# Attention on one Trainium2 core: half of the second pair additions move to VectorE, and the score and maximum matmuls become four column tiles of 32

## The chip, the core and the metric

The kernel runs on one core of a Trainium2 chip. A core has a matrix engine (TensorE; PE in the profile, PEld for its weight loads), VectorE (DVE), ScalarE (ACT), GpSimd (POOL) and SyncE (SP), which here only issues DMAs. The engines run apart from each other and meet at semaphores. The metric is the device time of one execution in microseconds (us); lower is better.

## What is computed

The reference chains three stages over a batch of 8 images of 384 channels by 1024 pixels: a convolution with correlations, attention, and an FFN. The change touches the attention alone. Cut to that:

```python
x = x + conv_ref(_gn(x), conv_w, conv_b)
t = to_tokens(x)                                  # (8, 1024, 384)
# attention of _ln_t(t): 12 heads of 32 channels
q, k, v = (heads(_ln_t(t) @ W.T) for W in (Wq, Wk, Wv))
scores = jnp.einsum('bhqd,bhkd->bhqk', q, k) * 32 ** -0.5
probs = jax.nn.softmax(scores, axis=-1)
out = jnp.einsum('bhqk,bhkd->bhqd', probs, v)
t = t + merge(out) @ Wo.T + bo
t = t + ffn_ref(_ln_t(t), in_weight, in_bias, out_weight)
```

## The kernel before

The attention of an image is cut into 24 **units**, `u` 0 to 23 (`IU`): 3 groups of 4 heads, and in each group 8 units (`w` = `u % 8`). A unit takes, for each of the 4 heads (steps `s` 0 to 3), 512 queries against 256 keys: two score tiles of 128 keys by 512 queries. Per unit there are so 8 score matmuls (`scores`, into the three PSUM banks `st`), 8 exponentials on ScalarE (`exponentials`, st to `ex`), and two calls of `weigh`, which multiply the exponentials of the unit before by v into `pv`. The softmax needs the maximum of each query's scores first, so every unit also has 8 matmuls of the scores the other way round for the next group (`max_scores`, into the two banks `mx`), and VectorE takes their maxima (`take_max`, line 1090). Item `i`'s matmul may only start when the maximum of item `i - 2` is taken, since it writes the same bank. In units with even `w` VectorE combines the maxima (`combine`) and PE transposes them (`turn`).

The sum of the exponentials is prepared by **pair additions**. For each step GpSimd adds the two halves of `ex` into `pair` (first addition, line 1445, 4 per unit). In an odd unit it also adds the `pair` of the even unit before it to that of this unit (second addition, line 1449, 4 per odd unit). `sum_up` on PE multiplies the result by ones, in the even unit that follows. In the last 8 units of the last image, where no maxima are left to take, VectorE makes the second additions (line 1174).

Beside this each unit carries a part of the next image's projections (units 6 to 23: `project_part`, 9 float16 matmuls in blocks of 5 and 4, or for v 36 short ones in blocks of 18 and 18) or of the last image's output projection (units 0 to 5: `out_project`, 9 in one block). Units 0 to 6 also hold the normalisation of the next image, units 21 and 23 its centring (`centre`); both are VectorE work. In every fourth unit (`u % 4 == 1`) VectorE inverts the sums (transpose, reciprocal, transpose).

The order on each engine is written out by hand: `unit(b, u)` in each engine's block. PE's is: scores of step 0, projection block, maximum 0, projection block, (`turn`), scores 1, maximum 1, `weigh`, maxima 2 and 3, scores 2, `weigh`, maximum 4, scores 3, maximum 5, (`sum_up` in even units), maxima 6 and 7. VectorE takes maxima 0 to 7 and does what `beside(n)` says ahead of maximum `n`. A hardware loop runs over images 0 to 5, from unit 6 of one image to unit 5 of the next.

A matmul whose output is 32 partitions wide, given a `tile_position`, uses a column tile of the array of 32 columns. `weigh` and `sum_up` work so, in groups of four (one tile for each head, float32; each shows as 8 matmuls in the trace). All the others use the whole array.

## Time and profile before

| | us |
|---|---|
| median of 3 runs | 3149.97 |
| lowest, highest | 3147.67, 3150.39 |
| the profiled execution | 3145.05 |
| its span, first to last instruction | 3143.1 |
| TensorE clock granted, mean of the span | 0.947 of full |

The span has the convolution up to about 400 us, the attention up to about 2330 us and the FFN after it. A page of the profile names work by line of the kernel, engine, operation and tiles (`b_mx<-b_kst,b_qst` writes the tile mx of the attention from kst and qst). Matmuls are pipelined: a float16 matmul of 512 moving columns is listed with 0.38 us, but the next one starts 0.216 us later, so that PE's load is read from the distance of starts, not from the busy time.

### The profile page before, as it was taken

What the parts mean: (1) busy time and instruction counts of PE and PEld (TensorE: products, weight loads), DVE (VectorE), ACT (ScalarE), POOL (GpSimd) and SP (SyncE); (2) the same over time, 40 slices, a digit from 0 to 9 for tenths busy, and PEclk for the clock granted to TensorE, in tenths of its full rate; (3) what the DMA queues carried; (4) which work ended last, traced back from release to release, by engine and by line L of the source; (5) the groups of instructions that cost most, each with busy time, mean ns of one, the idle gap of its engine ahead of it and who ended that gap; (6) DMA issues with size and microseconds to landing.
All of it is one profiled execution on the core that took longest, in us unless ns stands there. A gap on an engine that the chain in (4) does not pass through costs nothing. (4 is left out here: it accounts for less than half of the span.)

```text
span 3143.1 us, 52348 instructions
## 1 busy us (share of the span) xinstructions
PE 2819.9 (90%) x16784; PEld 1103.9 (35%) x16784; DVE 1900.0 (60%) x2871; ACT 1548.7 (49%) x2582; POOL 1849.4 (59%) x1407
## 2 busy tenths in 40 slices
PE   4988568999899899898998998999849999999999
PEld 3545231333233333332332332332114444444444
DVE  6766248777677677677677678776634333333332
ACT  3322023556556556556556556555634444444433
POOL 2323114899899899899899899999950111110110
PEclk8989776999999999999999999999989999999999
DMA  3333230021111211211211211112020011010110
GB/s 143 105 119 105 93 103 18 21 55 28 65 52 28 70 47 28 74 43 28 79 38 43 67 36 47 48 28 68 1 101 21 21 41 40 20 40 26 34 40 20
DMA packets 68754, 163.87 MB, mean 52 GB/s; under 512 B 13585, under 2 KB 17614, under 8 KB 67470
## 3 DMA queue, kind: packets, MB, share of 16 engines
q1 hardware_dynamic: 68494, 160.67, 16.0%
q8 instruction: 131, 2.15, 0.3%
q14 instruction: 129, 1.06, 0.1%
HBM read 59.20 MB, written 37.75 MB: 31 GB/s over the span
## 5 line engine op out<-in xcount | busy, mean ns | idle before, releaser
L1090 DVE TENSOR_REDUCE b_mxp<-b_mx 128x1 f32<-128x512 f32 x1536 | 1013.4, 684 | 445.7 <-PE b_mx L925 435.2
L1288 ACT ACTIVATE b_ex<-b_st 128x512 f32<-128x512 f32 x1536 | 828.1, 594 | 551.3 <-PE b_st L912 546.8
L1445 POOL TENSOR_TENSOR b_pair<-b_ex 128x512 f32<-128x512 f32 x768 | 987.0, 1296 | 144.1 <-ACT b_ex L1288 134.8
L925 PE MATMUL b_mx<-b_kst,b_qst 96*128 96x512 f16 x1536 | 561.8, 395 | 89.6 <-DVE b_mxp L1090 73.0
L1449 POOL TENSOR_TENSOR b_pair<-b_pair 128x512 f32<-128x512 f32 x368 | 491.5, 1336 | 28.9
L912 PE MATMUL b_st<-b_qst,b_kst 97*128 97x512 f16 x1536 | 473.5, 387 | 35.1 <-issue 17.7
L1665 DVE TENSOR_TENSOR c_gs<-c_g,c_gs 128x512 f16<-128x512 f32 x192 | 132.8, 692 | 481.9 <-ACT c_gs L1738 481.8
L1586 PE MATMUL c_hid<-c_z,c_wi 128*128 128x512 f16 x1728 | 405.6, 380 | 10.8 <-DVE c_z L1658 10.8
L946 PE MATMUL b_pv<-b_ex,b_v 128*32 128x512 f32 x3072 | 413.4, 611 | 1.0 <-ACT b_ex L1288 1.0
L1601 PE MATMUL c_acc<-c_gs,c_wo 128*128 128x512 f16 x1728 | 404.0, 379 | 0.1
L925 PEld LDWEIGHTS b_mx<-b_kst,b_qst 96*128 96x128 f16 x1536 | 130.0, 97 | 682.4 <-DVE b_mxp L1090 570.5
L1734 ACT ACTIVATE c_g<-c_hid,c_bias 128x512 f32<-128x512 f32 x192 | 131.4, 684 | 363.4 <-PE c_hid L1586 363.2
L1771 POOL TENSOR_TENSOR c_xs<-c_x 128x512 f32<-128x512 f32 x16 | 21.0, 1311 | 479.4 <-DMA c_x<-after_attention 479.4
L1586 PEld LDWEIGHTS c_hid<-c_z,c_wi 128*128 128x128 f16 x1728 | 169.4, 98 | 227.2 <-issue 19.2
L1601 PEld LDWEIGHTS c_acc<-c_gs,c_wo 128*128 128x128 f16 x1728 | 169.0, 98 | 204.2 <-ACT c_gs L1738 0.6
L912 PEld LDWEIGHTS b_st<-b_qst,b_kst 97*128 97x128 f16 x1536 | 149.6, 99 | 200.6 <-ACT b_ex L1288 50.3
L874 PE MATMUL b_pj<-b_z,b_wq 128*128 128x512 f16 x405 | 117.8, 422 | 21.7 <-issue 11.8
L524 POOL TENSOR_TENSOR a_sqs<-a_sq 128x1024 f32<-128x1024 f32 x8 | 18.8, 2355 | 200.3 <-ACT a_sq L502 200.3
L1738 ACT ACTIVATE c_gs<-c_g 128x512 f16<-128x512 f32 x192 | 120.9, 630 | 6.1
L1771 POOL TENSOR_TENSOR c_xs<-c_sq 128x512 f32<-128x512 f32 x16 | 20.3, 1268 | 168.7 <-ACT c_sq L1715 168.7
L1277 ACT ACTIVATE b_mr<-b_mx 8x128 f16<-8x128 f32 x96 | 25.5, 266 | 190.8 <-PE b_mx L931 190.8
L308 PE MATMUL a_conv<-a_fs,a_wm 128*128 128x512 f16 x432 | 117.1, 422 | 0.0
(159 smaller groups left out, 2897.1 us busy)
## 6 DMA issues: line engine op xcount, KB each, us to landing
a_x<-in_x SPq DMA_DIRECT2D x8, 1536.0 KB, 6.5
a_ob<-a_x SPq DMA_DIRECT2D x8, 1536.0 KB, 7.1
after_conv<-a_ob SPq DMA_DIRECT2D x24, 512.0 KB, 2.6
b_xl<-after_conv SPq DMA_DIRECT2D x8, 1536.0 KB, 6.4
b_qst<-b_staged0q SPq DMA_DIRECT2D x192, 64.0 KB, 2.0
b_kst<-b_staged0k SPq DMA_DIRECT2D x192, 64.0 KB, 2.0
b_v<-b_vstaged SPq DMA_DIRECT2D x24, 512.0 KB, 3.0
b_xr<-after_conv SPq DMA_DIRECT2D x8, 1536.0 KB, 6.6
```

The lines of the kernel that those rows point to most:

```text
L912: nc.tensor.matmul(st[(SCORES * u + n) % NST][:, :], kst[g][0:MAXROW + 1, s, kt * P:(kt + 1) * P], qst[g][0:MAXROW + 1, s, half * BANK:(ha ...
L925: nc.tensor.matmul(mx[item % 2][:, :], qst[g][0:MAXROW, h, t * P:(t + 1) * P], kst[g][0:MAXROW, h, half * BANK:(half + 1) * BANK], start=T ...
L946: last = nc.tensor.matmul(pv[h * HEAD:(h + 1) * HEAD, :], v[g][:, kt, h * HEAD:(h + 1) * HEAD], ex[u % 2 * HG + h][:, e * BANK:(e + 1) * B ...
L1090: nc.vector.reduce_max(mxp[h % 2][:, t, half:half + 1], mx[item % 2][:, :], AX_X).then_inc(mx_taken, 1)
L1288: nc.scalar.activation(ex[u % 2 * HG + s][:, e * BANK:(e + 1) * BANK], st[(SCORES * u + n) % NST][:, :], ACT.Exp, scale=SCALE).then_inc(ex ...
L1445: nc.gpsimd.tensor_tensor(both[:, :], e[:, 0:BANK], e[:, BANK:NPIX], ALU.add).then_inc(pair_ready, 1)
L1449: nc.gpsimd.tensor_tensor(both[:, :], both[:, :], pair[s][:, :], ALU.add).then_inc(pair_added, 1)
L1586: last = nc.tensor.matmul(hid[m % NH][:, :], wi[a][:, k, m * P:(m + 1) * P], z[p][b][:, k, :], start=n == 0, stop=n == 8)
L1601: last = nc.tensor.matmul(acc[j][:, :], wo[a][:, m, j * P:(j + 1) * P], gs[m % NS][b][:, :], start=m == 0 and n == 0, stop=m == MC - 1 and ...
L1665: nc.vector.tensor_tensor(gs[m % NS][1][:, :], g[m % NG][:, :], gs[m % NS][0][:, :], ALU.subtract).then_inc(glo_ready, 1)
L1734: nc.scalar.activation(g[m % NG][:, :], hid[m % NH][:, :], ACT.Gelu, bias=bias[:, m:m + 1], scale=1.0 / WSCALE).then_inc(gelu_ready, 1)
L1738: nc.scalar.activation(gs[m % NS][0][:, :], g[m % NG][:, :], ACT.Copy).then_inc(ghi_ready, 1)
```

## The change

Two things. First, in odd units that have maxima, the second additions of steps 0 and 1 are taken from GpSimd and given to VectorE, which makes them ahead of maxima 5 and 7 (`add_pair`, in `beside`). Those of steps 2 and 3 stay on GpSimd. There are now two semaphores `pair_added`, one for steps 0 and 1 and one for steps 2 and 3, and `sum_up` waits for both. Second, each matmul of `scores` and `max_scores` becomes four, each for 32 of the 128 output partitions, with `tile_position=(0, c)`; only the last of the four signals. The columns of weights that they load are 32 instead of 128; each streams the same 512 moving columns.

```diff
--- before.py
+++ after.py
@@ -684,7 +684,7 @@
         st_ready = N.sem("st_ready")
         exp_ready = N.sem("exp_ready")
         pair_ready = N.sem("pair_ready")
-        pair_added = N.sem("pair_added")
+        pair_added = [N.sem(f"pair_added{e}") for e in range(2)]
         pv_ready = N.sem("pv_ready")
         sum_ready = N.sem("sum_ready")
         pv_moved = N.sem("pv_moved")
@@ -731,6 +731,9 @@
             if i < first:
                 return range(0)
             return range((i - first) * each, (i - first + 1) * each if i < NQKV - 1 else ITEMS)
+
+        def added(b, u, s):
+            return STEPS // 2 * (IU // 2 * b + u // 2) + s + 1
 
         def turn_of(b, u):
 
@@ -909,10 +912,12 @@
                     kt = 2 * kp + e
                     n = 2 * s + e
                     wait(pe, exp_ready, SCORES * (IU * b + u) + n + 1 - NST)
-                    nc.tensor.matmul(st[(SCORES * u + n) % NST][:, :],
-                                     kst[g][0:MAXROW + 1, s, kt * P:(kt + 1) * P],
-                                     qst[g][0:MAXROW + 1, s, half * BANK:(half + 1) * BANK],
-                                     start=True, stop=True).then_inc(st_ready, 1)
+                    for c in range(0, P, HEAD):
+                        last = nc.tensor.matmul(st[(SCORES * u + n) % NST][c:c + HEAD, :],
+                                                kst[g][0:MAXROW + 1, s, kt * P + c:kt * P + c + HEAD],
+                                                qst[g][0:MAXROW + 1, s, half * BANK:(half + 1) * BANK],
+                                                start=True, stop=True, tile_position=(0, c))
+                    last.then_inc(st_ready, 1)
 
             def max_scores(group, m, g, item):
                 h, t, half = item // (2 * TILES), item // 2 % TILES, item % 2
@@ -922,9 +927,12 @@
                     wait(pe, row_ready, HG * group + h)
                 if item == 0:
                     pe.wait_ge(stacked[g], STACKED * (m + 1))
-                nc.tensor.matmul(mx[item % 2][:, :], qst[g][0:MAXROW, h, t * P:(t + 1) * P],
-                                 kst[g][0:MAXROW, h, half * BANK:(half + 1) * BANK],
-                                 start=True, stop=True).then_inc(mx_ready, 1)
+                for c in range(0, P, HEAD):
+                    last = nc.tensor.matmul(mx[item % 2][c:c + HEAD, :],
+                                            qst[g][0:MAXROW, h, t * P + c:t * P + c + HEAD],
+                                            kst[g][0:MAXROW, h, half * BANK:(half + 1) * BANK],
+                                            start=True, stop=True, tile_position=(0, c))
+                last.then_inc(mx_ready, 1)
 
             def turn(number, parity):
                 pe.wait_ge(combined, number + 1)
@@ -953,7 +961,8 @@
             def sum_up(b, u):
 
                 w = u % UNITS
-                pe.wait_ge(pair_added, STEPS // 2 * (IU * b + u + 1))
+                for e in range(2):
+                    pe.wait_ge(pair_added[e], added(b, u, STEPS // 2 - 1))
                 if w % 4 == 1:
                     if u >= 4:
                         pe.wait_ge(sum_inverted, INVERSE * (6 * b + u // 4) - 2)
@@ -1109,6 +1118,12 @@
                 if quarter == 2:
                     dve.wait_ge(sum_inverted, at + 2)
                     nc.vector.transpose(inv[:, :], over_columns(inv_col)).then_inc(sum_inverted, 1)
+
+            def add_pair(b, u, s):
+                dve.wait_ge(pair_ready, STEPS * (IU * b + u) + s + 1)
+                both = pair[HG + s]
+                nc.vector.tensor_tensor(both[:, :], both[:, :], pair[s][:, :], ALU.add
+                                        ).then_inc(pair_added[s // 2], 1)
 
             def attended(b, x):
                 dve.wait_ge(sum_inverted, INVERSE * (6 * b + x + 1))
@@ -1169,13 +1184,12 @@
                     if maxima:
                         take_max(group, 8 * w + 2 * s + e)
                     elif u % 2 and e == 1:
-                        dve.wait_ge(pair_ready, STEPS * (IU * b + u) + s + 1)
-                        both = pair[HG + s]
-                        nc.vector.tensor_tensor(both[:, :], both[:, :], pair[s][:, :], ALU.add
-                                                ).then_inc(pair_added, 1)
+                        add_pair(b, u, s)
 
                 def beside(n):
 
+                    if maxima and u % 2 and n in (5, 7):
+                        add_pair(b, u, n // 2 - 2)
                     if not maxima:
                         if u % 4 == 1 and n == 0:
                             for quarter in range(4):
@@ -1440,14 +1454,15 @@
                         wait(pool, sum_ready, IU // 2 * b + u // 2)
                     if u % 2 == 0 and not (isinstance(b, int) and b == 0 and u == 0):
 
-                        pool.wait_ge(pair_added, STEPS // 2 * (unit_no - 2) + s + 1)
+                        pool.wait_ge(pair_added[s // 2], added(*((b, u - 1) if u else (b - 1, IU - 1)),
+                                                               s % 2))
                     e, both = ex[u % 2 * HG + s], pair[u % 2 * HG + s]
                     nc.gpsimd.tensor_tensor(both[:, :], e[:, 0:BANK], e[:, BANK:NPIX], ALU.add
                                             ).then_inc(pair_ready, 1)
-                    if u % 2 and maxima:
+                    if u % 2 and s >= 2 and maxima:
                         pool.wait_ge(pair_ready, STEPS * unit_no + s + 1)
                         nc.gpsimd.tensor_tensor(both[:, :], both[:, :], pair[s][:, :], ALU.add
-                                                ).then_inc(pair_added, 1)
+                                                ).then_inc(pair_added[1], 1)
 
             def epilogue(b):
                 attended_low(b, 5)
```

On VectorE the end of unit 9 reads so before, from maximum 3 to the combined maximum (names: mxp partial maxima, inv the inverted sums, nm the combined maxima):

```order
L1090 TENSOR_REDUCE b_mxp0<-b_mx1 128x1
L1090 TENSOR_REDUCE b_mxp0<-b_mx0 128x1
L1090 TENSOR_REDUCE b_mxp0<-b_mx1 128x1
L1090 TENSOR_REDUCE b_mxp0<-b_mx0 128x1
L1111 STREAM_TRANSPOSE b_inv<-b_inv_col 128x512
L1090 TENSOR_REDUCE b_mxp0<-b_mx1 128x1
L1096 TENSOR_REDUCE b_nm0<-b_mxp0 128x8
```

and now:

```order
L1099 TENSOR_REDUCE b_mxp0<-b_mx1 128x1
L1099 TENSOR_REDUCE b_mxp0<-b_mx0 128x1
L1125 TENSOR_TENSOR b_pair4<-b_pair4,b_pair0 128x512
L1099 TENSOR_REDUCE b_mxp0<-b_mx1 128x1
L1099 TENSOR_REDUCE b_mxp0<-b_mx0 128x1
L1125 TENSOR_TENSOR b_pair5<-b_pair5,b_pair1 128x512
L1120 STREAM_TRANSPOSE b_inv<-b_inv_col 128x512
L1099 TENSOR_REDUCE b_mxp0<-b_mx1 128x1
L1105 TENSOR_REDUCE b_nm0<-b_mxp0 128x8
```

Ahead of maximum 5 and ahead of maximum 7 stands now an addition; nothing else of VectorE's moves.

On GpSimd an odd unit reads so before:

```order
L1445 TENSOR_TENSOR b_pair4<-b_ex4 128x512
L1449 TENSOR_TENSOR b_pair4<-b_pair4,b_pair0 128x512
L1445 TENSOR_TENSOR b_pair5<-b_ex5 128x512
L1449 TENSOR_TENSOR b_pair5<-b_pair5,b_pair1 128x512
L1445 TENSOR_TENSOR b_pair6<-b_ex6 128x512
L1449 TENSOR_TENSOR b_pair6<-b_pair6,b_pair2 128x512
L1445 TENSOR_TENSOR b_pair7<-b_ex7 128x512
L1449 TENSOR_TENSOR b_pair7<-b_pair7,b_pair3 128x512
```

and now:

```order
L1460 TENSOR_TENSOR b_pair4<-b_ex4 128x512
L1460 TENSOR_TENSOR b_pair5<-b_ex5 128x512
L1460 TENSOR_TENSOR b_pair6<-b_ex6 128x512
L1464 TENSOR_TENSOR b_pair6<-b_pair6,b_pair2 128x512
L1460 TENSOR_TENSOR b_pair7<-b_ex7 128x512
L1464 TENSOR_TENSOR b_pair7<-b_pair7,b_pair3 128x512
```

The second additions of pair4 and pair5 are gone, those of pair6 and pair7 stand where they stood.

On PE the first two thirds of unit 9 read so before (pj projection, st scores, mx maxima, pv `weigh`; 32x512 is a column tile):

```order
L874 MATMUL b_pj<-b_z,b_wk 128x512 x5
L925 MATMUL b_mx<-b_kst,b_qst 128x512
L874 MATMUL b_pj<-b_z,b_wk 128x512 x4
L912 MATMUL b_st<-b_qst,b_kst 128x512 x2
L925 MATMUL b_mx<-b_kst,b_qst 128x512
L946 MATMUL b_pv<-b_ex,b_v 32x512 x4
L925 MATMUL b_mx<-b_kst,b_qst 128x512 x2
L912 MATMUL b_st<-b_qst,b_kst 128x512 x2
L946 MATMUL b_pv<-b_ex,b_v 32x512 x4
```

and now:

```order
L877 MATMUL b_pj<-b_z,b_wk 128x512 x5
L931 MATMUL b_mx<-b_kst,b_qst 32x512 x4
L877 MATMUL b_pj<-b_z,b_wk 128x512 x4
L916 MATMUL b_st<-b_qst,b_kst 32x512 x8
L931 MATMUL b_mx<-b_kst,b_qst 32x512 x4
L954 MATMUL b_pv<-b_ex,b_v 32x512 x4
L931 MATMUL b_mx<-b_kst,b_qst 32x512 x8
L916 MATMUL b_st<-b_qst,b_kst 32x512 x8
L954 MATMUL b_pv<-b_ex,b_v 32x512 x4
```

The order is the same; each whole matmul of st and mx has become four column tiles, and the projection's blocks (x5, x4) are what is left of the whole array.

## Rows read from the trace of the kernel before

**Rows 1.** The page, busy time: us, share of the span, instructions.
```profile
PE 2819.9 (90%) x16784; PEld 1103.9 (35%) x16784; DVE 1900.0 (60%) x2871; ACT 1548.7 (49%) x2582; POOL 1849.4 (59%) x1407
```
**Rows 2.** Windows: length, busy us (instructions) by engine, clock, DMA share, GB/s.
```profile
1278.28:1391.51 113.23, 109.95 (x696) 39.19 (x695) 81.76 (x132) 66.78 (x130) 101.91 (x82) 1.00 0.16 45
1304.10:1313.20 9.10, 9.01 (x78) 3.90 (x77) 6.60 (x11) 5.47 (x11) 9.02 (x8) 1.00 0.01 3
1295.70:1304.10 8.40, 8.00 (x42) 2.58 (x41) 6.99 (x13) 4.84 (x10) 7.24 (x7) 1.00 0.00 0
1239.10:1251.70 12.60, 11.66 (x62) 3.88 (x60) 12.54 (x18) 7.00 (x12) 12.16 (x9) 1.00 0.01 2
1263.20:1278.30 15.10, 12.04 (x52) 3.37 (x51) 8.09 (x14) 5.49 (x12) 8.54 (x7) 0.74 0.43 160
2110.00:2250.00 140.00, 129.20 (x694) 35.68 (x691) 96.48 (x158) 81.71 (x158) 135.89 (x109) 0.96 0.12 39
```
**Rows 3.** Waits in 1278 to 1391 us: us in total, times, longest.
```profile
PEld b_mx L925 <- DVE b_mxp L1090: 35.1, 46, 0.8
...
POOL b_pair L1445 <- ACT b_ex L1288: 9.4, 12, 1.4
```
**Rows 4.** Timeline, PE, unit 9 of image 3: start us, length us, operation.
```profile
1295.31 0.60 PE L912 MATMUL b_st<-b_qst,b_kst 97*128 97x512 f16 x2
...
1298.35 0.38 PE L925 MATMUL b_mx<-b_kst,b_qst 96*128 96x512 f16 x1
1298.65 1.07 PE L946 MATMUL b_pv<-b_ex,b_v 128*32 128x512 f32 x8
1299.65 0.60 PE L925 MATMUL b_mx<-b_kst,b_qst 96*128 96x512 f16 x2
...
1301.62 0.39 PE L925 MATMUL b_mx<-b_kst,b_qst 96*128 96x512 f16 x1
...
1303.45 0.39 PE L925 MATMUL b_mx<-b_kst,b_qst 96*128 96x512 f16 x1 [0.26 <-DVE b_mxp L1090]
1303.67 0.60 PE L912 MATMUL b_st<-b_qst,b_kst 97*128 97x512 f16 x2
```
**Rows 5.** Timeline, DVE, the end of the same unit.
```profile
1301.29 2.70 DVE L1090 TENSOR_REDUCE b_mxp<-b_mx 128x1 f32<-128x512 f32 x4
...
1305.31 0.17 DVE L1096 TENSOR_REDUCE b_nm<-b_mxp 128x8 f32<-128x16 f32 x1
1305.49 1.03 DVE L1116 TENSOR_TENSOR b_pvs<-b_pvs,b_inv 128x512 f32<-128x512 f32 x1
```
**Rows 6.** The page, costliest groups: count, busy us, mean ns, idle before them.
```profile
L1445 POOL TENSOR_TENSOR b_pair<-b_ex 128x512 f32<-128x512 f32 x768 | 987.0, 1296 | 144.1 <-ACT b_ex L1288 134.8
...
L1449 POOL TENSOR_TENSOR b_pair<-b_pair 128x512 f32<-128x512 f32 x368 | 491.5, 1336 | 28.9
```
**Rows 7.** Groups by shape, DVE, 2150 to 2400 us: the pair additions there.
```profile
L1174 DVE TENSOR_TENSOR b_pair<-b_pair 128x512 f32<-128x512 f32 x16 | 26.0, 1685 | 15.5 <-POOL b_pair L1445 15.5
```
**Rows 8.** Timeline, PE, FFN: float32 between float16 matmuls, whole array.
```profile
2380.96 1.02 PE L1567 MATMUL c_stat<-c_xs,c_mean_w 128*128 128x512 f32 x2
2381.82 2.11 PE L1586 MATMUL c_hid<-c_z,c_wi 128*128 128x512 f16 x9
```
**Rows 9.** Timeline, PE, convolution: 144 matmuls of 32 moving columns.
```profile
153.26 3.77 PE L271 MATMUL a_gram<-a_fn 128*128 128x32 f16 x144
```
**Rows 10.** Timeline at 1504 us: weight loads and matmuls of one column-tiled group.
```profile
1504.20 0.16 PEld L946 LDWEIGHTS b_pv<-b_ex,b_v 128*32 128x32 f32 x8 [0.24 <-issue]
1504.21 1.06 PE L946 MATMUL b_pv<-b_ex,b_v 128*32 128x512 f32 x8
```
**Rows 11.** Timeline, DVE, unit 4 of image 3.
```profile
1245.60 1.79 DVE L1065 TENSOR_TENSOR b_xl<-b_xl,b_xs 128x512 f32<-128x512 f32 x1
```
**Rows 12.** Timeline, PE, the first matmul after the loop's branch.
```profile
1262.55 1.03 PE L912 MATMUL b_st<-b_qst,b_kst 97*128 97x512 f16 x2 [3.24 <-issue]
```

## The prediction

> **What bounds the kernel now.** I read the busy times first, then windows over single stretches of the attention, then the waits in one of them, then single units on PE and VectorE. The page shows PE with 90% of the span, VectorE with 60%, GpSimd with 59% [rows 1]; but GpSimd works almost only in the attention, and there it looks full: 101.91 of 113.23 us in 13 regular units (7 to 19 of image 3), 135.89 of 140 us in the last image [rows 2]. The change takes work from it, so the first question is whether anyone waits for it. In the regular units nobody does: GpSimd itself waits 9.4 us for exponentials, while the long waits are PE's weight loads on a taken maximum, 35.1 us [rows 3]. 13 units in 113.23 us are 8.71 us each; an even unit takes 9.1 and an odd one 8.4 us [rows 2], 17.4 us a pair.
>
> Unit 9 on PE shows why. It runs from 1295.31 to 1303.67 [rows 4], 8.36 us. Its load by distance of starts: 16 score and maximum matmuls and 9 of the projection at 0.216 us are 5.40 us; each of two `weigh` groups adds 1.09 us (the maximum ahead starts at 1298.35, the one behind at 1299.65, less its own 0.216). That is 7.6 us. The other 0.75 us are at the unit's end: maximum 7's matmul may start at 1303.45 only, when VectorE has taken maximum 5 [rows 4]. VectorE takes maxima 3 to 6 without a pause from 1301.29, four in 2.70 us [rows 5]. So PE binds for most of a unit, and VectorE in the last third of an odd one. This is just where the additions are put in.
>
> **The additions on VectorE.** 92 odd units have maxima (184 units with maxima in all), so 184 additions move. GpSimd loses 184 x 1.336 = 246 us [rows 6]; as nobody waits for it in the regular units, I count that as nothing there. On VectorE maximum 4 is taken up 0.43 us behind its matmul's start at 1301.62 [rows 4], which the column tiles leave about where it is (below), and takes 0.68 us [rows 5]. Then comes the first addition, D us long, then maximum 5, and only then may PE issue maximum 7, and behind it in PE's queue the next unit's scores, projection and all. In numbers from the unit's start: maximum 4 taken at 7.4, addition to 7.3 + D, maximum 5 taken at 7.95 + D, the next unit at 8.23 + D, against 8.36 now: an odd unit grows by D - 0.13. The second addition stands ahead of maximum 7; PE meets it at the next `turn`, which waits for the combined maximum. That comes now at 1305.31, with `turn` some 1.0 us behind, and PE's own delay by D covers the rest, so a regular unit hides it.
>
> What is D? The trace has this addition on VectorE 16 times, mean 1.685 us, in a stretch where GpSimd never pauses [rows 7]. VectorE's other operations on two float32 tiles in SBUF take 1.03 us in unit 10 [rows 5] and 1.79 us in unit 4 [rows 11], while operations on a tile in PSUM always take 0.68: the SBUF ones wait for GpSimd's running operation. So D lies between 0.68 and 1.79. GpSimd's load in a regular pair falls from 12 additions to 10, some three quarters of the time; I take **D = 1.1**, nearest to the 1.03 of the neighbouring unit. Both additions' other wait, for the first addition by GpSimd (`pair_ready`), is met: GpSimd makes those of steps 0 and 1 in the first two thirds of the unit.
>
> **The column tiles.** Does a group of four still take 0.216 us? The float32 groups of `weigh` say yes: eight matmuls of four tiles are done in 1.06 us [rows 10], about what two float32 matmuls of the whole array take (1.02 us) [rows 8]. Enough instructions pass: 144 loads and matmuls of 32 columns in 3.77 us are 26 ns a pair [rows 9], four pairs 105 ns. What a group costs over its streaming is the change of tile shape. 1.09 us against 0.86 us for two float32 matmuls (1567 to the next line, 2380.96 to 2381.82, which also shows that float32 beside float16 costs nothing) [rows 4, 8] leave 0.23 us for going in and out, 0.115 a change. Before, an odd unit has 4 changes, an even one 6 with `sum_up`. After, scores, maxima, `weigh` and `sum_up` have one shape, and only the blocks of the projection differ: 4 changes in either. So an odd unit keeps its time, and an even one gains 0.23, with a little of a shorter stall behind `turn` 0.3 us.
>
> The skill has a rule that speaks against this. Rows 10 show all eight weight loads done within 0.16 us, while the second four matmuls cannot start before the first four have streamed for 0.43 us: loads run beside matmuls of the same rows. The Trainium skill, "TensorE: Matmul & The Clock Gate", Part 3, says that a weight load overlaps a running matmul only where its row group differs; four column tiles share all rows, and by that rule every group would show its loads. The rows don't bear it out, so it is a rival (below) and no term.
>
> **The sum**, by units:
> - Regular pairs: odd +0.97, even -0.3: +0.67 a pair. 49 pairs of units 7 to 20 in images 0 to 6 and 4 more: 53 x 0.67 = +35. Bounds +0.25 (D = 0.68) and +1.85 (D = 1.79 and stalls at `turn`).
> - Units 21 and 23 with the centring, where VectorE's queue is full to the end, and `turn` waits for it: both additions count, 2.2 - 0.3 = 1.9 each, 12 units: +23 (14 to 38).
> - Units 3 and 5 with the normalisation. Unit 4 shows VectorE with 12.54 of 12.60 us [rows 2], so all that is added ahead of it is paid: 2.4 us in unit 3; in unit 5 only the first addition, 1.2, since the loop's branch hides the rest. For unit 1, which waits for ScalarE more than for VectorE, an estimate of 0.3. Seven images: 3.9 x 7 = +27 (13 to 42).
> - The loop's branch. PE waits 3.24 us for nothing in the kernel [rows 12], in a stretch at 160 GB/s and a clock of 0.74 [rows 2]; I take it for the fetching of instructions. The maxima and scores need four times as many now, so I put +1 us on each of 6 passages: +6 (0 to 24).
> - The other even units: -2.
> - The last image, units 6 to 15: GpSimd has 135.89 of 140 us [rows 2], so here it does bind, and losing 2 of 12 additions a pair gives back some 1.3 us until VectorE binds: -6 (-10 to 0).
>
> Together 35 + 23 + 27 + 6 - 2 - 6 = **+83 us**. The profiled execution took 3145.05 us, 4.9 less than the median 3149.97; on the median this gives **3233 us**, 2.6% slower. The bounds add up to about +30 and +200: 3180 to 3350.
>
> **The rivals.**
> - *GpSimd sets the pace after all.* For it: 97% busy in units such as unit 4 and in the last image [rows 2]. Against it: in the regular units it waits for exponentials. If it held every pair, its 2.67 us less would be limited by what PE has to give, the 0.75 us at the odd unit's end, 0.3 in the even one: about 1.0 x 92 = 90 us faster, 3060. It decides if the additions on VectorE find D near 0.7 and `turn` never waits. Chance 0.17; its times reach from 3040 to 3143.
> - *Nearly nothing.* The additions fall into GpSimd's gaps (D = 0.7), and going from tiles to the whole array costs nothing, as only the other direction has to drain. Then a regular pair is 0.2 us faster, units 3, 5, 21, 23 cost some 25 us, the last image gives 10: 3150 to 3165. Chance 0.14, of which 0.05 within 0.2%.
> - *The weight loads are not hidden.* Eight loads end in 0.16 us, so four in some 0.13 [rows 10]; 3072 groups in the units x 0.13 are 399 us, of which the stalls behind VectorE swallow a part: with the forecast's terms about 3500. Chance 0.06. This is what the skill's rule would give.
> - *Dearer groups or fetching.* Each group costs a few ns more (0.03 x 3072 = 92 us), or PE waits for instructions in other busy stretches too: 3330 to 3450. Chance 0.06.
> - The forecast: 0.57, from 3170 to 3330.
>
> **How the numbers follow.** A measurement of this kernel can tell some 0.2%, 6 us, from no change. Faster by more than that: the first rival, 0.17. Within: 0.05. Slower: 0.57 + 0.09 + 0.06 + 0.06 = 0.78. From 3120 to 3340 us I leave out most of the first rival (0.11) and the dear cases (0.09).
>
> **What would show it.** In the profile after: VectorE's pair additions with a mean of 1.0 to 1.2 us; in a regular odd unit PE's maximum 7 starting right behind the taking of maximum 5, and the unit 9.2 to 9.5 us long; even units 8.7 to 8.8; the pair 18.1 instead of 17.4. GpSimd below 80% in the regular units and waiting for exponentials more often. Between a projection block and a maximum 0.33 instead of 0.216 us from start to start, around `weigh` nothing over streaming. Wrong would be: four tiles further apart than 0.22 us from the next four; a mean of the additions above 1.5 us, which goes to the upper bound; odd units no longer than 8.5, which would mean that VectorE had room that I don't see; and a loop's branch with more than two restarts.

## The result, and the profile after

The changed kernel takes **3266.55 us** (median of 4 runs, 3263.51 to 3269.13) against 3150.18 us of the kernel before beside it (4 runs, 3147.67 to 3151.92): a ratio of 1.0374, with a 95% interval of 1.0361 to 1.0386. It is 3.7% slower, 116 us; forecast were 83 us, 3233 us with a range of 3120 to 3340. The direction and the mechanism of the odd units were right. The parts of the sum were not: two of them were far too small, two too large. The profiled execution of after has a span of 3261.7 us, that of before 3143.1: 118.6 us to explain.

First the page of after: the busy times, then the costliest groups that the change touches (count, busy us, mean ns, idle time before them and what ended it).

```profile
PE 2832.4 (87%) x26000; PEld 1175.4 (36%) x26000; DVE 2113.8 (65%) x3055; ACT 1553.1 (48%) x2582; POOL 1679.0 (51%) x1223
...
L1460 POOL TENSOR_TENSOR b_pair<-b_ex 128x512 f32<-128x512 f32 x768 | 1005.9, 1316 | 400.8 <-ACT b_ex L1302 397.6
...
L1464 POOL TENSOR_TENSOR b_pair<-b_pair 128x512 f32<-128x512 f32 x184 | 285.7, 1553 | 14.4
L1125 DVE TENSOR_TENSOR b_pair<-b_pair 128x512 f32<-128x512 f32 x200 | 271.9, 1364 | 12.0 <-POOL b_pair L1460 12.0
```

Against [rows 1, 6]: PE's busy share fell from 90% to 87% though it issues 26000 matmuls instead of 16784; its busy time grew by 12.5 of the 118.6 us, and most of the time that came is PE waiting. GpSimd lost 170 us of work and its wait for exponentials grew from 134.8 to 397.6 us, a first sign that its work was not what the others waited for. VectorE's 200 additions (16 of them, those of the last units, were VectorE's before) have a mean of 1.364 us, where 1.0 to 1.2 was forecast, and GpSimd's own second additions grew from 1.336 to 1.553 us each.

Three units of image 3 in windows (length, busy us of each engine, clock, DMA share, GB/s): unit 8, unit 9 and unit 10.

```profile
1335.90:1346.30 10.40, 10.40 (x102) 3.42 (x98) 7.31 (x11) 5.59 (x12) 7.29 (x6) 0.84 0.00 0
1346.30:1355.60 9.30, 7.97 (x93) 2.79 (x89) 7.77 (x14) 4.84 (x10) 6.08 (x6) 1.00 0.01 2
1355.60:1365.40 9.80, 9.19 (x129) 4.37 (x125) 8.46 (x12) 5.48 (x11) 8.22 (x7) 1.00 0.02 4
```

The same unit 9 took 8.40 us before, and an even unit 9.10 [rows 2]. Measured from the start of each unit's first exponential to that of the next, all units fall into a few kinds, and one table carries most of what follows. Images count from 0; "im." is image, and the last one is image 7. Units 7 to 20 are "regular"; units 21 to 23 of image 6 hold no centring and are counted with them below. The right half gives the sum of the differences to the kernel before, over all units of that kind.

```
                        length of one, us              sum of the differences to before, us
                   before  after  tiles  additions    after   tiles   additions
                                  alone  alone                alone   alone
odd 7 to 19          8.4    9.3    8.4     9.1        +45.7    -0.3     +34.5
8, 12, 16, 20        9.1    8.7    8.7     9.4         -4.4   -10.5      +8.8
10, 14, 18           9.1   10.0    8.8    10.3        +19.5    -6.7     +25.3
21 to 23 (im. 0-5)   9.4    9.9    9.4                 +9.5    +0.4     +12.4
21 to 23 (im. 6)                                       +2.8    -0.5      +2.7
0 to 6 (im. 0-6)                                      +23.7    -8.2     +39.5
last image          179    195    179     199         +15.7    +0.1     +19.6
all units                                            +112.5   -25.7    +142.8
```

The odd units are the forecast, and PE shows why. Its timeline at the end of unit 9 and into unit 10 (start us, length us, operation, idle time before it and what ended it):

```profile
1349.31 0.39 PE L931 MATMUL b_mx<-b_kst,b_qst 96*32 96x512 f16 x4
1349.53 1.03 PE L954 MATMUL b_pv<-b_ex,b_v 128*32 128x512 f32 x8
1350.39 0.60 PE L931 MATMUL b_mx<-b_kst,b_qst 96*32 96x512 f16 x8
...
1353.37 0.40 PE L931 MATMUL b_mx<-b_kst,b_qst 96*32 96x512 f16 x4 [0.20 <-DVE b_mxp L1099]
1354.90 0.40 PE L931 MATMUL b_mx<-b_kst,b_qst 96*32 96x512 f16 x4 [1.14 <-DVE b_mxp L1099]
1355.13 0.61 PE L916 MATMUL b_st<-b_qst,b_kst 97*32 97x512 f16 x8
...
1358.70 0.27 PE L939 MATMUL b_mx<-b_ident,b_nm 128*8 128x128 f32 x1 [0.41 <-DVE b_nm L1105]
```

The first three lines are a maximum, a group of `weigh` and the next maximum. From maximum to group is 0.22 us, from group to maximum 0.86 us, which is bare streaming; in [rows 4] the same way took 0.30 and 1.00. The fifth line is maximum 7. Its wait is 1.14 us where it was 0.26 [rows 4], and it ends with VectorE's taking of maximum 5. The difference, 0.88, is nearly all of the odd unit's growth (0.93). The last line is the `turn`, and it waits 0.41 us for the combined maximum: by the forecast it would not.

VectorE in the same stretch, then GpSimd:

```profile
1353.23 1.01 DVE L1125 TENSOR_TENSOR b_pair<-b_pair 128x512 f32<-128x512 f32 x1
1354.17 1.28 DVE L1099 TENSOR_REDUCE b_mxp<-b_mx 128x1 f32<-128x512 f32 x2
1355.37 1.79 DVE L1125 TENSOR_TENSOR b_pair<-b_pair 128x512 f32<-128x512 f32 x1
1357.08 0.70 DVE L1120 STREAM_TRANSPOSE b_inv<-b_inv_col 128x512 f32<-128x512 f32 x1
1357.71 0.65 DVE L1099 TENSOR_REDUCE b_mxp<-b_mx 128x1 f32<-128x512 f32 x1
1358.47 0.17 DVE L1105 TENSOR_REDUCE b_nm<-b_mxp 128x8 f32<-128x16 f32 x1
1358.66 1.40 DVE L1131 TENSOR_TENSOR b_pvs<-b_pvs,b_inv 128x512 f32<-128x512 f32 x1
```
```profile
1352.43 1.27 POOL L1460 TENSOR_TENSOR b_pair<-b_ex 128x512 f32<-128x512 f32 x1 [0.66 <-ACT b_ex L1302]
1353.78 1.60 POOL L1464 TENSOR_TENSOR b_pair<-b_pair 128x512 f32<-128x512 f32 x1
1355.34 1.27 POOL L1460 TENSOR_TENSOR b_pair<-b_ex 128x512 f32<-128x512 f32 x1
```

The two additions are not alike. The first starts 0.47 us before a GpSimd operation of 1.27 us ends (1353.70) and is itself done at 1354.24. The second starts 0.03 us behind the start of another one and waits it out whole: GpSimd's ends at 1356.61, VectorE's at 1357.16. Both end 0.54 to 0.55 us behind GpSimd's. The other way round it is the same: GpSimd's operation at 1353.78 takes 1.60 us instead of 1.27, and VectorE's first addition ends 0.46 us into it. That the second one falls so badly is no chance. Both engines go on from the end of the first, 1354.24: GpSimd's next operation starts 1.10 us later, VectorE's second addition 1.13. In all 49 regular odd units of images 0 to 6 the second takes 1.77 to 1.79 us, whatever the first took (1.01 to 1.17).

### The profile page after: what moved, and what is told of

It is laid out like the page before. It is cut to its first block and busy times, and to the rows that moved or that the text cites. A ratio compares the mean times of both kernels' runs of the same rounds, so it can differ in the third digit from the quotient of the medians.

```text
span 3261.7 us, 70865 instructions
## 1 busy us (share of the span) xinstructions
PE 2832.4 (87%) x26000; PEld 1175.4 (36%) x26000; DVE 2113.8 (65%) x3055; ACT 1553.1 (48%) x2582; POOL 1679.0 (51%) x1223
## 5 line engine op out<-in xcount | busy, mean ns | idle before, releaser
L1460 POOL TENSOR_TENSOR b_pair<-b_ex 128x512 f32<-128x512 f32 x768 | 1005.9, 1316 | 400.8 <-ACT b_ex L1302 397.6
L931 PE MATMUL b_mx<-b_kst,b_qst 96*32 96x512 f16 x6144 | 585.9, 398 | 174.9 <-DVE b_mxp L1099 170.2
L916 PE MATMUL b_st<-b_qst,b_kst 97*32 97x512 f16 x6144 | 490.2, 391 | 44.3 <-issue 27.8
L931 PEld LDWEIGHTS b_mx<-b_kst,b_qst 96*32 96x32 f16 x6144 | 166.3, 95 | 714.3 <-DVE b_mxp L1099 565.1
L1464 POOL TENSOR_TENSOR b_pair<-b_pair 128x512 f32<-128x512 f32 x184 | 285.7, 1553 | 14.4
L1125 DVE TENSOR_TENSOR b_pair<-b_pair 128x512 f32<-128x512 f32 x200 | 271.9, 1364 | 12.0 <-POOL b_pair L1460 12.0
L916 PEld LDWEIGHTS b_st<-b_qst,b_kst 97*32 97x32 f16 x6144 | 153.9, 97 | 237.3 <-ACT b_ex L1302 92.5
L954 PEld LDWEIGHTS b_pv<-b_ex,b_v 128*32 128x32 f32 x3072 | 97.4, 112 | 70.8 <-issue 7.8
```

The costliest lines, as they stand in the source:

```text
L916: last = nc.tensor.matmul(st[(SCORES * u + n) % NST][c:c + HEAD, :], kst[g][0:MAXROW + 1, s, kt * P + c:kt * P + c + HEAD], qst[g][0:MAXRO ...
L931: last = nc.tensor.matmul(mx[item % 2][c:c + HEAD, :], qst[g][0:MAXROW, h, t * P + c:t * P + c + HEAD], kst[g][0:MAXROW, h, half * BANK:(h ...
L954: last = nc.tensor.matmul(pv[h * HEAD:(h + 1) * HEAD, :], v[g][:, kt, h * HEAD:(h + 1) * HEAD], ex[u % 2 * HG + h][:, e * BANK:(e + 1) * B ...
L1125: nc.vector.tensor_tensor(both[:, :], both[:, :], pair[s][:, :], ALU.add).then_inc(pair_added[s // 2], 1)
L1460: nc.gpsimd.tensor_tensor(both[:, :], e[:, 0:BANK], e[:, BANK:NPIX], ALU.add).then_inc(pair_ready, 1)
L1464: nc.gpsimd.tensor_tensor(both[:, :], both[:, :], pair[s][:, :], ALU.add).then_inc(pair_added[1], 1)
```

## The experiments

All ratios are to the kernel before, measured beside. "Changed kernel" is the one of this change.

**The two halves apart.** With the tiles alone, the additions go back to GpSimd:

```diff
-                    if maxima and u % 2 and n in (5, 7):
-                        add_pair(b, u, n // 2 - 2)
...
-                    if u % 2 and s >= 2 and maxima:
+                    if u % 2 and maxima:
```

> The changed kernel with the second additions of steps 0 and 1 back on GpSimd; only the column tiles are left of the change. My theory: the tiles cost nothing in odd units and give 0.3 us in even ones, so the time is some 25 us under the kernel before, 3115 to 3140. Rival 1, the tiles cost something of their own (weight loads that show, dearer groups, fetching of instructions): 3160 to 3260, and the additions are then not the cause of the slowdown. Rival 2, GpSimd paces the kernel: 3150, since its work is as before.

Measured: 3124.75 us (3119.00 to 3129.73), ratio 0.9919 (0.9898 to 0.9939). The odd unit's end is as short as before:

```profile
1294.40 0.40 PE L931 MATMUL b_mx<-b_kst,b_qst 96*32 96x512 f16 x4 [0.20 <-DVE b_mxp L1099]
1295.01 0.40 PE L931 MATMUL b_mx<-b_kst,b_qst 96*32 96x512 f16 x4 [0.20 <-DVE b_mxp L1099]
```

A change of tile shape costs what the prediction said, and by its count an even unit now has fewer of them. In the changed kernel a whole-array block starts 0.33 us behind the maximum ahead of it, where a column-tiled group starts 0.22 us behind it:

```profile
1356.78 0.40 PE L931 MATMUL b_mx<-b_kst,b_qst 96*32 96x512 f16 x4
1357.11 1.18 PE L887 MATMUL b_pj<-b_wv,b_z 128*128 128x128 f16 x18
```

With the additions alone, scores and maxima are matmuls of the whole array again:

```diff
-                for c in range(0, P, HEAD):
-                    last = nc.tensor.matmul(mx[item % 2][c:c + HEAD, :],
...
+                nc.tensor.matmul(mx[item % 2][:, :], qst[g][0:MAXROW, h, t * P:(t + 1) * P],
```

> The changed kernel with whole-array matmuls for scores and maxima; only the two additions on VectorE are left of the change. My theory: they are the whole cause, and the tiles had paid some of it back: 3275 to 3300. If the tiles were the cause: 3140 to 3180. If GpSimd's relief is worth something that the tiles took away: under 3150.

Measured: 3292.43 us (3291.48 to 3293.42), ratio 1.0453 (1.0435 to 1.0470). The halves add up: -25.7 and +142.8 us of units make +117.1, and together they give +112.5. So the tiles are worth 25 us, and the additions cost some 140. In the table the tiles' gain is where the forecast put it: 49 regular even units gain 17.2 us, 0.35 each (forecast 0.3), and the odd ones nothing. With the additions alone the first addition of a regular odd unit takes 0.83 us in images 0 to 5 (it meets GpSimd later in its operation), the odd unit grows by 0.70, which is the forecast's D - 0.13, and the second addition takes 1.77 to 1.78 all the same.

**Does anyone wait for GpSimd?** In the kernel before, the second additions of steps 0 and 1 are left out, and with them the waits for them:

```diff
-                    if u % 2 and maxima:
+                    if u % 2 and s >= 2 and maxima:
```

> The kernel before, with the second additions of steps 0 and 1 left out altogether in the units with maxima (nobody makes them, so the sums lack these parts); 184 additions, 246 us of GpSimd's work, are gone. My theory: nobody waits for GpSimd in the regular units, so it stays at 3150, at most 15 us less by the last image. Rival, GpSimd sets the pace: some 90 us less, 3060.

Measured: 3158.66 us (3155.01 to 3161.41), ratio 1.0024 (1.0013 to 1.0036). Regular units keep their 8.4 and 9.1 us to the tenth; the last image gives 9 us back, and units 5 and 6 around the loop's branch take 13 us more, which neither theory had. GpSimd's wait for exponentials in image 3, before and with the additions left out:

```profile
POOL b_pair L1445 <- ACT b_ex L1288: 12.9, 16, 1.5
```
```profile
POOL b_pair L1462 <- ACT b_ex L1301: 46.4, 42, 4.4
```

Of the 24 additions that an image no longer has, 32 us at 1.336 each, 33.5 us came back as waiting. The first rival, that GpSimd sets the pace, is refuted outside the last image. It also bounds what relieving GpSimd of these additions can bring in this kernel: nothing but the last image's 9 us.

**One addition at either place.** Only step 0's addition is VectorE's, ahead of maximum 5 or ahead of maximum 7; steps 1 to 3 are GpSimd's. Both have the tiles. The edit for maximum 5:

```diff
-                    if maxima and u % 2 and n in (5, 7):
-                        add_pair(b, u, n // 2 - 2)
+                    if maxima and u % 2 and n == 5:
+                        add_pair(b, u, 0)
...
-                    if u % 2 and s >= 2 and maxima:
+                    if u % 2 and s >= 1 and maxima:
```

> The changed kernel with only step 0's second addition on VectorE, ahead of maximum 5; steps 1 to 3 stay on GpSimd. Column tiles as in the change. My theory: this one gates maximum 7's matmul and with it the next unit, so every odd unit is some 9.3 us instead of 8.4 with the tiles alone, the even ones 8.7; over the kernel with the tiles alone (3125) 53 x 0.9, units 21 and 23 12 x 1.0, units 3 and 5 some 14, last image some 7: 3205 to 3215. Rival, only VectorE's total work counts: half of what both additions cost over the tiles alone, 3190 to 3200.

Measured: 3315.79 us (3314.92 to 3318.74), ratio 1.0521 (1.0503 to 1.0539). That is 100 us beyond the expectation, and slower than the changed kernel with both additions.

> The changed kernel with only one second addition (step 0's) on VectorE, ahead of maximum 7. My theory: PE does not wait for it in the odd unit (8.4 us, as with the tiles alone); it only delays the combined maximum, which shows in units with u % 4 == 2, where the sums' inversion is queued behind it (9.6 to 9.9 us instead of 8.8), and in the last image, where no projection hides the turn. 3175 to 3195. Rival: it shows in all odd units alike, 9.3 us, 3205 and more.

Measured: 3136.12 us (3134.69 to 3142.05), ratio 0.9957 (0.9942 to 0.9972). That is 40 to 60 us better than expected: the same work, two maxima later, is 180 us cheaper. Regular units are 8.4 and 8.6 to 8.9 us, about as with the tiles alone. Unit 22 grows, from 9.2 to 11.0, which is 11 us over six images and as much as the whole kernel's difference to the tiles alone; units 0 to 2 and 10, 14 and 18 give some 10 us more together, and the last image and units 3 to 6 about as much back.

The additions' lengths give the first half of the reason. Shortest, median and longest from 1330 to 1440 us, ahead of maximum 5 and ahead of maximum 7:

```profile
L1126 DVE TENSOR_TENSOR b_pair<-b_pair x5: 1155/1654/1722, 1336.1 to 1422.2; 128x512 f32<-128x512 f32 x5
```
```profile
L1126 DVE TENSOR_TENSOR b_pair<-b_pair x6: 679/687/1757, 1336.8 to 1428.5; 128x512 f32<-128x512 f32 x6
```

Ahead of maximum 5 it starts 0.16 us behind a GpSimd operation and waits it out:

```profile
1381.54 1.26 POOL L1461 TENSOR_TENSOR b_pair<-b_ex 128x512 f32<-128x512 f32 x1
1381.70 1.65 DVE L1126 TENSOR_TENSOR b_pair<-b_pair 128x512 f32<-128x512 f32 x1
```

Ahead of maximum 7 the two start within 0.02 us of each other, VectorE takes its bare 0.68 us, and GpSimd pays, with 1.83 us:

```profile
1302.61 1.83 POOL L1465 TENSOR_TENSOR b_pair<-b_pair 128x512 f32<-128x512 f32 x1
1302.63 0.68 DVE L1126 TENSOR_TENSOR b_pair<-b_pair 128x512 f32<-128x512 f32 x1
```

In the changed kernel a start 0.03 us behind GpSimd's lost a whole operation, here one 0.02 us behind won. The recorded starts do not tell who goes first in so close a case. The Trainium skill, "SBUF — State Buffer", section "SBUF: two separate sides", describes an exclusive lock: a VectorE operation with two SBUF inputs and a GpSimd operation that reads SBUF take the same pair of ports, the earlier holds it for its whole length, and the other is blocked. The rows agree in all but the exact start: 0.68 and 1.27 us bare, 1.01 to 1.79 and 1.60 to 1.83 where they meet.

The second half is PE's clock. PE behind that addition, in the kernel with one addition ahead of maximum 5, then windows over the same time (the clock is the third number from the end):

```profile
1384.02 0.44 PE L932 MATMUL b_mx<-b_kst,b_qst 96*32 96x512 f16 x4 [1.77 <-DVE b_mxp L1100]
1384.24 1.07 PE L917 MATMUL b_st<-b_qst,b_kst 97*32 97x512 f16 x8
1385.24 2.10 PE L888 MATMUL b_pj<-b_wv,b_z 128*128 128x128 f16 x18
1387.27 0.57 PE L932 MATMUL b_mx<-b_kst,b_qst 96*32 96x512 f16 x4
1387.77 1.18 PE L888 MATMUL b_pj<-b_wv,b_z 128*128 128x128 f16 x18
```
```profile
1382.00:1384.00 2.00, 0.24 (x4) 0.00 (x0) 2.00 (x3) 0.33 (x1) 1.92 (x2) 1.00 0.00 0
1384.00:1385.20 1.20, 1.18 (x12) 0.37 (x12) 1.20 (x3) 0.28 (x1) 1.20 (x2) 0.60 0.00 0
1385.20:1387.30 2.10, 2.10 (x26) 1.87 (x22) 1.97 (x3) 0.81 (x2) 2.02 (x3) 0.50 0.03 8
```

Behind an idle time of 1.77 us PE runs for 3 us at half its clock, 1.2 instead of 2.4 GHz: the first block of 18 takes 2.10 us, the second 1.18. In 46 of the 49 regular odd units the clock fell within 3.5 us behind this wait. So the odd unit costs 1.6 us more (9.9 to 10.5), and the even unit behind it another 1.4 (mostly 9.9 to 10.4): a pair takes 20.2 us instead of 17.2.

**Is it the place, or what GpSimd does there?** The last kernel keeps the addition ahead of maximum 5 and takes GpSimd's work from that stretch:

```diff
-                    if u % 2 and s >= 1 and maxima:
+                    if u % 2 and s == STEPS - 1 and maxima:
```

> The kernel with one addition on VectorE ahead of maximum 5 (step 0's), and of the three second additions that were left to GpSimd those of steps 1 and 2 made by nobody (184 additions left out, so the sums of exponentials lack a part in the units with maxima); step 3's stays. In the kernel that makes them all, GpSimd starts on an operation 0.16 us ahead of VectorE's addition, the addition takes 1.65 us, PE then idles 1.77 us and its granted clock is 0.5 to 0.6 for 3 us behind it; a pair takes 20.2 us. Theory: an addition on VectorE that meets a running GpSimd operation waits for its end, and the idle time that this makes costs the clock too. With GpSimd idle at that point: additions 0.68 to 0.75 us, odd units 8.9 to 9.1, granted clock 1.00 throughout, even units 8.6 to 8.9, a pair 17.8; 53 pairs x 2.4 = 127 us less than 3316, and some 15 to 20 less in the units 21 to 23: 3165 to 3195 us. Rival, it is the place ahead of maximum 5 that costs, not what GpSimd does: additions still 1.5 or more or the clock still at half behind them, pairs of 19.5 or more, 3270 to 3316 us.

Measured: 3219.76 us (3218.52 to 3228.78), ratio 1.0234 (1.0217 to 1.0252), 96 us below its neighbour. The additions, and one of them beside GpSimd:

```profile
L1125 DVE TENSOR_TENSOR b_pair<-b_pair x6: 1015/1017/1084, 1340.0 to 1430.4; 128x512 f32<-128x512 f32 x6
```
```profile
1339.21 1.27 POOL L1461 TENSOR_TENSOR b_pair<-b_ex 128x512 f32<-128x512 f32 x1 [0.67 <-ACT b_ex L1303]
...
1340.01 1.02 DVE L1125 TENSOR_TENSOR b_pair<-b_pair 128x512 f32<-128x512 f32 x1
```

The direction is as the theory has it: the same place, less GpSimd, and the addition falls from 1.65 to 1.02, PE's wait from 1.77 to 1.13, and the clock stays whole behind it in most units; the even unit returns to 8.6 to 8.8. But it did not fall to 0.68, since a first addition of GpSimd now runs there (1339.21 to 1340.48; VectorE's again ends 0.55 behind it). Odd units of 9.3 instead of 8.9 to 9.1 us are 10 to 20 of the 25 to 55 us by which the time misses its range; the clock gives some 18 more. In 12 of the 49 regular even units the clock fell all the same (10.2 to 10.4 us), behind waits as long as in the others, 1.1 to 1.3 us. The changed kernel has four such units: unit 8 in images 2 to 4 (clock 0.84 and 10.3 us in the window above, 8.8 us in images 0, 1 and 5) and unit 12 of image 6; in units 10, 14 and 18 of image 0 the clock cost some 0.4 us each. The length of the wait alone does not decide it: with both additions ahead of maximum 7 (below) the `turn` waits 1.4 to 1.5 us in 21 regular units, and the clock fell behind none of them. What decides stayed open.

**Where the second addition costs.** By the forecast a regular unit hides it, but units 10, 14 and 18 grew by 0.9 us against before and 1.2 against the tiles alone. These units also hold the inversion (L1120) and `attended` (L1131). Step 1's addition is put behind the combined maximum instead:

```diff
-                    if maxima and u % 2 and n in (5, 7):
-                        add_pair(b, u, n // 2 - 2)
+                    if maxima and u % 2 and n == 5:
+                        add_pair(b, u, 0)
+                    if (u % 2 == 0 and n == 1 and not (isinstance(b, int) and b == 0 and u == 0)
+                            and (maxima or u == IU - UNITS)):
+                        add_pair(*((b, u - 1) if u else (b - 1, IU - 1)), 1)
```

> The changed kernel, but VectorE makes the addition of step 1 ahead of maximum 1 of the next even unit, behind the combined maximum, instead of ahead of maximum 7 of the odd unit; step 0's stays ahead of maximum 5. Theory: what the second addition costs in the regular units comes through the combined maximum: in units 10, 14 and 18, which also hold the inversion of the sums and the multiplication by it, it makes the combined maximum, with it the turn, the multiplication and ScalarE behind it late, 1.2 us a unit. Expected: units 10, 14, 18 back at 8.6 to 8.9, odd units still 9.3, so 24 x 1.2 = 29 us less in the regular units; units 1, 3, 5 and 19 get longer by 1 to 2 us each because VectorE waits there for GpSimd's first addition, as with both additions placed late (about +5 an image); total 3225 to 3245 us. Rival, VectorE simply has too much work between an odd unit's maxima and the multiplication, whatever the order: units 10, 14, 18 stay at 9.8 to 10.2, total 3265 to 3275.

Measured: 3243.87 us (3241.71 to 3248.10), ratio 1.0288 (1.0271 to 1.0305). The total is within what was expected, the units are between the two theories: 10, 14 and 18 take 9.4 us. The `turn` waits no longer, as forecast, but VectorE has no gap from 1347 to 1357.6, and its maxima are late behind it:

```profile
1353.75 0.27 PE L939 MATMUL b_mx<-b_ident,b_nm 128*8 128x128 f32 x1
...
1356.47 0.40 PE L931 MATMUL b_mx<-b_kst,b_qst 96*32 96x512 f16 x4 [0.44 <-DVE b_mxp L1099]
```

About half of the 1.2 us was the late combined maximum. The other half stays with the addition behind it; by these rows it is VectorE's load. In most of the other even units (8.8 to 8.9) the second addition costs nothing to 0.3; in five of them the clock fell and they took 10.2 to 10.3.

Then both additions ahead of maximum 7:

```diff
-                    if maxima and u % 2 and n in (5, 7):
-                        add_pair(b, u, n // 2 - 2)
+                    if maxima and u % 2 and n == 7:
+                        add_pair(b, u, 0)
+                        add_pair(b, u, 1)
```

> The changed kernel, but both of VectorE's additions stand ahead of maximum 7; none ahead of maximum 5. Theory of the prediction: the addition ahead of maximum 5 lengthens the odd unit because maximum 7's matmul waits for maximum 5; an addition ahead of maximum 7 meets only the turn. Expected: odd units 8.4 as with the tiles alone; even units pay for a later combined maximum: 8.8 goes to 9.2 to 9.8, and units 10, 14, 18 to 10.5 to 11.2; a pair 18.3 to 18.8, total 3240 to 3275 us. Rival, what counts is VectorE's load and not the place: odd units 9.3, total as the changed kernel, 3262 to 3270 with the same unit lengths. Second rival: two additions in a row start while GpSimd works and each waits for a whole operation (1.79 each), turn waits over 1.5 us and the clock falls behind it as in the kernel with one addition ahead of maximum 5: 3290 or more.

Measured: 3262.28 us (3258.46 to 3268.46), ratio 1.0347 (1.0328 to 1.0366). Here the time alone would have misled: it is that of the changed kernel, as the rival has it, but the units are not. Odd ones are 8.4 us, even ones 9.7 to 9.8, units 10, 14 and 18 10.9 to 11.1, at or just above what the theory gave. The additions take 2.84 us together and the `turn` pays them, with the clock still at 1.00 from 1330 to 1440 us:

```profile
1352.67 2.84 DVE L1125 TENSOR_TENSOR b_pair<-b_pair 128x512 f32<-128x512 f32 x2
```
```profile
1357.05 0.27 PE L939 MATMUL b_mx<-b_ident,b_nm 128*8 128x128 f32 x1 [1.46 <-DVE b_nm L1105]
```

So an addition ahead of maximum 5 is paid by the odd unit, two ahead of maximum 7 by the even one, and one ahead of maximum 7, if it is short, by nobody in the regular units: there is room at that place for 0.68 us, not for 2.84.

**Both additions late.** Step 0's ahead of maximum 1 of its own unit, step 1's ahead of maximum 1 of the next even one, with the tiles:

```diff
-                    if maxima and u % 2 and n in (5, 7):
-                        add_pair(b, u, n // 2 - 2)
+                    if maxima and u % 2 and n == 1:
+                        add_pair(b, u, 0)
...
```

The lines left out are those of step 1 in the even unit, as above.

> The changed kernel with the same two additions on VectorE in other places: step 0's ahead of maximum 1 of the odd unit, where VectorE waits some 1.0 us and GpSimd has just finished, and step 1's ahead of maximum 1 of the even unit that follows, where VectorE waits some 1.7 us. My theory: what cost the time is the place ahead of maxima 5 and 7, not the amount, so this gives 3110 to 3150. Rival, VectorE's amount of work counts (1.1 to 1.4 us in every unit): 3220 to 3270, as the changed kernel.

Measured: 3211.80 us (3208.83 to 3220.86), ratio 1.0205 (1.0183 to 1.0227), over 60 us above the range. In units 7 to 18 it did what was expected, 8.4 and 8.6 to 8.8 us as with the tiles alone, fully hidden. The rest was a new wait that I had not priced. Near the start of an odd unit GpSimd must have made step 0's first addition already; where it also normalises or folds (units 1, 3, 5, 19, up to 16.1 us) it has not, and the maxima behind the addition on VectorE wait too. VectorE in unit 1 of image 3, and GpSimd ahead of it:

```profile
1244.04 1.74 DVE L1125 TENSOR_TENSOR b_pair<-b_pair 128x512 f32<-128x512 f32 x1 [1.74 <-POOL b_pair L1463]
```
```profile
1238.92 1.26 POOL L1412 TENSOR_TENSOR b_xs<-b_z 128x512 f32<-128x512 f32 x1
1240.26 1.26 POOL L1415 TENSOR_TENSOR b_xs<-b_xs,b_z 128x512 f32<-128x512 f32 x1
1241.49 3.73 POOL L1463 TENSOR_TENSOR b_pair<-b_ex 128x512 f32<-128x512 f32 x3
```

**The last image.** The changed kernel with the last image's additions back on GpSimd:

```diff
-                    if maxima and u % 2 and n in (5, 7):
+                    if (maxima and u % 2 and n in (5, 7)
+                            and not (isinstance(b, int) and b == n_images - 1)):
...
-                    if u % 2 and s >= 2 and maxima:
+                    if u % 2 and maxima and (s >= 2 or isinstance(b, int) and b == n_images - 1):
```

> The changed kernel, but in the last image (units 5 to 15 there have the moved additions) all four second additions are GpSimd's, as before; images 0 to 6 keep two of them on VectorE. Theory: the last image is a term of its own. There no projection stands between the odd unit's end and the turn, so the wait for the combined maximum shows in full: the last image takes 195 us in the changed kernel and 179 with the tiles alone. Expected: last image about 179, total 3266 - 16 = 3250 us (3246 to 3255), the other images unchanged. Rival, the last image is long because of what the images before it leave behind (stores, code, a lower clock), not because of its own additions: total 3260 to 3270 and the last image still 190 or more.

Measured: 3249.42 us (3245.30 to 3254.50), ratio 1.0306 (1.0288 to 1.0323), last image 180 us: as expected. This image has no projection between the odd unit's end and the `turn`, so the wait is bare, and the clock goes with it. Over the image PE waits 14.7 us for combined maxima and 13.2 us for maxima in the changed kernel, 3.8 and 2.6 with the tiles alone. VectorE, PE, and windows over the clock:

```profile
2310.44 1.78 DVE L1125 TENSOR_TENSOR b_pair<-b_pair 128x512 f32<-128x512 f32 x1
...
2313.46 0.17 DVE L1105 TENSOR_REDUCE b_nm<-b_mxp 128x8 f32<-128x16 f32 x1
```
```profile
2313.68 0.38 PE L939 MATMUL b_mx<-b_ident,b_nm 128*8 128x128 f32 x1 [2.65 <-DVE b_nm L1105]
...
2315.24 1.92 PE L954 MATMUL b_pv<-b_ex,b_v 128*32 128x512 f32 x8
```
```profile
2313.60:2317.00 3.40, 3.32 (x25) 0.94 (x29) 2.72 (x4) 1.87 (x4) 2.05 (x2) 0.50 0.00 1
```

**Two attempts at a faster kernel.** The tiles alone, with the finished image's store held back until the next image's unit 6, to see whether the loop's branch is slow because of the store:

```diff
                 sp.wait_ge(o_added, 6 * b + 6)
+                sp.wait_ge(exp_ready, SCORES * (IU * (b + 1) + FIRST + 1))
```

> The kernel with the tiles alone (3125), and the store of the finished image and the load behind it held back until the next image's unit 6 has its exponentials, so that no data is moved while PE restarts behind the loop's branch. If the collision of these transfers with the fetching of instructions makes the branch long: units 5 and 6 together 20 to 22 instead of 24 us, 3100 to 3115. If the branch has a length of its own: 3120 to 3130.

Measured: 3131.44 us (3125.15 to 3136.96), ratio 0.9943 (0.9925 to 0.9960). Units 5 and 6 take 24 us together as before: the store is not what makes the branch long.

The tiles alone, with VectorE making steps 0 and 1 in the last image only, ahead of maxima 1 and 3 of the even unit, where GpSimd does bind:

```diff
+                    if (isinstance(b, int) and b == n_images - 1 and u % 2 == 0 and FIRST < u <= IU - UNITS
+                            and n in (1, 3)):
+                        add_pair(b, u - 1, n // 2)
...
```

> The kernel with the tiles alone (3125), and only in the last image's units 7 to 15, where GpSimd is full, the second additions of steps 0 and 1 on VectorE, made in the even unit behind, ahead of maxima 1 and 3. If GpSimd paces these units: some 6 to 10 us less, 3115 to 3119. If VectorE's waiting for GpSimd eats it: 3125 or more.

Measured: 3122.25 us (3120.93 to 3124.72), ratio 0.9908 (0.9892 to 0.9925). The last image takes 173 instead of 179 us, but the totals of this kernel and of the tiles alone lie within each other's ranges. It is the fastest one run, 0.9% below the kernel before, and nearly all of that is the tiles. The time stayed above the 3115 to 3119 us that were expected.

## Why the prediction was right or wrong

By its own terms, against the 118.6 us of the two profiled spans:

- **Regular units: forecast +35 and -2, measured +63.6** (with units 21 to 23 of image 6). *The first addition* was right: D taken as 1.1, measured 1.01; an odd unit to grow by 0.97, measured 0.93. Its working, D - 0.13, held in other kernels too: 0.70 at D = 0.83, and 1.6 against 1.52 at D = 1.65. The bounds 0.68 and 1.79 were both met in the runs, and they are not noise but the two ends of one thing: VectorE comes first, or it waits for GpSimd's operation to end, whole or what is left of it. *The tiles* were right as well (0.35 a regular even unit), and nothing over streaming around `weigh`, as the timeline shows. *"A regular unit hides it"*, said of the second addition, is the step that failed. It took the second addition to be as long as the first, D, and PE's delay to cover it. It was 1.79 us, because both engines go on together from the end of the first one, and GpSimd's next operation starts 0.03 us ahead. And I looked at one unit only: in every second even unit VectorE also has the inversion and `attended`, and there is no room. The kernel with the second addition moved showed that half of it is order; the other half is put down to load. Units 10, 14 and 18 gave +19.5 us where -6 was expected.
- **Last image: forecast -6, measured +15.7**, the other step that failed. The relief of GpSimd is real (9 us with the additions left out), but "until VectorE binds" came at once: without projection blocks the `turn` waits 2.65 us, PE's clock halves behind it, and 25 us are lost. The run with this image's additions back on GpSimd gave 17 us back.
- **Units 21 to 23: forecast +23, measured +9.5.** "VectorE's queue is full to the end" was too strong: the three units grew by 0.5 us on average, not two of them by 1.9. The additions take 1.0 and 1.35 us there, near the 2.2 that the forecast took for both; what hid the rest was not followed up.
- **Units 0 to 6: forecast +27 and +6 for the branch, measured +23.7.** Units 3 and 4 gave 16.7, 0 to 2 gave 6.1, 5 and 6 together 0.9. These numbers hide more than they show. The 16.7 us look like the forecast's 2.4 in seven images, but units 3 and 4 grow by 9.7 us with the tiles alone and by 17.2 with the additions alone, so the agreement is partly luck. Units 5 and 6 gain 16 us with the tiles alone, lose 19 with the additions alone and 13 when additions are merely left out. So the branch's term had the wrong reason: with the tiles alone PE has four times the matmuls for scores and maxima, and its longest wait in units 5 and 6 of images 1 to 5 stays at 3.3 to 3.5 us (3.2 to 4.0 before); it is 4.7 to 6.5 in the changed kernel and 5.9 to 6.2 with the additions left out. What makes the branch so sensitive stayed open; the store is excluded.
- **The clock**: it fell in unit 8 of three images and in unit 12 of one, about 6 us of the 63.6, and cost about 1 us in units 10, 14 and 18 of image 0. I had no term for the clock in the regular units at all.
- Outside the units some 6 us were added, which I did not follow up.

The differences are +31, +22, -13, -9 and +6, together the 36 us between forecast and measured span. The errors partly cancelled, so the total looks better than its parts.

Of the rivals, "GpSimd sets the pace" is refuted by the additions left out and "the weight loads are not hidden" by the tiles alone, which are 25 us faster than the kernel before, and by the groups of maxima and `weigh`, which stand 0.22 and 0.86 us apart in the changed kernel. "Nearly nothing" needed D near 0.7. The run with one addition ahead of maximum 7 comes near that case, at 0.9957: it needs one addition instead of two, and in the other place.

## What to carry to other kernels

Before work goes from one engine to another, ask who waits for the engine that is relieved; leaving the work out answers it in one run, and here the answer was nobody outside the last image. An operation on two SBUF tiles on VectorE has no one length beside a busy GpSimd: 0.68 us or up to 1.79, by the instant at which it starts, so a move of two instructions can change the price of both. Where two of them stand near each other, the first can set the phase in which the second meets GpSimd. Where PE is the bound, count a wait not only by its length but by what the clock does behind it, and look at all kinds of units of a loop, not at one.
